# Mamba stage of a Trainium2 kernel: loop nest replaced by one list of stages with lags per engine

## The chip, the cores and the metric

The kernel runs on one NeuronCore of one Trainium2 chip. The metric is the device time of one execution in microseconds (us), lower is better. The kernel before takes 4172.57 us, the median of 3 runs (4169.62 to 4175.07). The engines are TensorE (PE, matmul), VectorE (DVE), ScalarE (ACT), GpSimd (POOL) and SyncE (SP). Each runs its own queue strictly in the order in which it was written, and they meet only at semaphores.

## The reference

The input x is (4, 1024, 128) in float32. A layer norm and a bidirectional Mamba block come first, then a transformer of 6 layers. The change is in the Mamba block alone, which computes this for a forward and for a backward (flipped) direction:

```
xp, z = split(x @ W_in.T)                      # 256 channels each
xc = silu(depthwise_conv4(xp) + b_conv)
dt, B, C = split(xc @ W_x.T)                   # 8, 16 and 16 columns
dt = softplus(dt @ W_dt.T + b_dt)
A = -exp(A_log)
# over 1024 tokens, for each of 256 channels and 16 states n:
h = h * exp(dt * A[n]) + (dt * xc) * B[n]
y = sum_n h * C[n]
y = (y + xc * D) * silu(z)
out = y @ W_out.T                              # x + 0.5 * (forward + backward)
```

## The kernel before

`program` (L1283 on) runs two layer norms, then `mamba` (L101), a third layer norm, and `transformer` (L588), each in a block of its own. The last two are the same in both kernels.

`mamba` works in 8 passes, one for each sequence (4) and direction (2). In a pass the tokens lie along the free dimension (1024) and the channels on the partitions, in two halves h of 128. A pass has 16 steps, one for each state n, and `g` counts steps through all passes (128 in all). One step is:

- PE spreads row B[n] over 128 partitions into a pair of PSUM banks (`b_rows`) and row C[n] into the other pair (`c_rows`). Both are the instruction of L209, two matmuls of 512 columns each.
- DVE forms the drive of half 0 in SBUF (L393) and that of half 1 in place in PSUM (L395), and scans each half over 1024 tokens (L411, `tensor_tensor_scan`, 128x1024).
- ACT has computed exp(dt * A[n]) for both halves up to 4 steps ahead (`decays`, L309) and copies the C row to SBUF (L316).
- POOL multiplies state by C row (L425), and PE adds this product to y in PSUM by a matmul with the identity (`add_read`, L229), four matmul instructions of 512 columns in the trace for each half.

PSUM has 8 banks: 4 hold y of the two halves, and the other 4 are two "slots" of two banks. B of step g takes slot g % 2; everything else of that step (C rows, every projection, the output) takes the other slot, two banks at a time. Whoever takes a slot waits for its last reader. So B of step g + 1 waits for whatever last read that slot in step g.

The next pass's projections are spread over the steps of this pass by the table `PROJECT_AT`: x at steps 1, 4 and 6, B/C/dt at 8, dt of each half at 9 and 10, z at 12 and 13. An x part of one bank is four taps, in the trace eight matmul instructions of 512 columns (L182); step 1 has two such banks. PE's order within a step is written in the loop: C rows, `add_read` of half 0 of the step before, output or projection, `add_read` of half 1, then B rows of the next step. ACT evaluates silu straight from PSUM (L277 for x, L281 for z) in each of five steps, among the exponentials, so tables are reloaded both ways (ACT_TABLE_LOAD). At step 1 DVE closes the pass before (`gate`): L366 adds xc * D to y, reading PSUM, and L372 multiplies by silu(z). At step 2 PE projects the output (L238) and DVE adds it to the residual (L380).

## Time and profile before

| | us |
|---|---|
| median of 3 runs | 4172.57 |
| the profiled execution | 4178.99 |
| its span | 4176.9 |
| first drive of step 0 (L393) starts | 115.22 |
| last scan (L411) ends | 1217.45 |
| last add to the residual (L380) starts | 1231.12 |

A time is read as us from the start of the span. A row of a group of instructions has its busy time, the mean of one in ns, the number (x), and, behind the bar, how long the engine sat idle just before such instructions and who ended that. One float32 matmul of 512 columns appears as two MATMUL instructions. The Mamba stage takes the first 1232 of 4177 us; the rest is the third norm and the transformer.

### The profile page before, as it was taken

To read this page: it belongs to the slowest core of one execution; us is meant where nothing else is said; L and a number is where in the kernel's file an instruction comes from. 1 tells how busy PE (TensorE), PEld (TensorE's weight loads), DVE (VectorE), ACT (ScalarE), POOL (GpSimd) and SP (SyncE) were. 2 spreads that over 40 slices of the span, in tenths; PEclk is the share of its full clock that TensorE was granted. 3 is DMA by queue.
4 is the path that set the end of the run, shared out by engine and by line. 5 is a ranking of instruction groups with operands and counts; after the bars stand their busy time and mean duration, and the time that the engine had idled before them with its cause. 6 is when DMAs were issued, how large, how long until landed. Compare 5 with 4: busy or idle time off the path is not lost.

```text
span 4176.9 us, 110200 instructions
## 1 busy us (share of the span) xinstructions
PE 3828.7 (92%) x43616; PEld 2570.0 (62%) x43616; DVE 3409.8 (82%) x3480; ACT 3048.1 (73%) x6956; POOL 3035.9 (73%) x2330
## 2 busy tenths in 40 slices
PE   6788888888875999999999999999999999999998
PEld 2333333333333777777777777777777777777775
DVE  3788888888975888788887888788887888788885
ACT  4655645564534888788887888788887888788885
POOL 0455555554546888888888888888888888888883
PEclk8888898898887999999999999999999999999999
DMA  1000000000000000000000000000000000000001
GB/s 41 0 1 0 0 0 0 0 0 0 0 20 32 13 2 15 2 6 13 15 3 2 16 2 15 2 6 12 2 15 2 16 2 15 2 6 2 3 2 42
DMA packets 12012, 34.46 MB, mean 8 GB/s; under 512 B 2405, under 2 KB 4329, under 8 KB 10609
## 3 DMA queue, kind: packets, MB, share of 16 engines
q1 hardware_dynamic: 11504, 27.41, 1.9%
q8 instruction: 353, 5.78, 0.6%
q14 instruction: 155, 1.26, 0.1%
HBM read 23.21 MB, written 4.19 MB: 7 GB/s over the span
## 4 chain that ended last, share of the span: by engine, by line
PE 64%; issue 2%; ACT 1%; POOL 1%; DVE 0%; POOLq 0%; ACTq 0%; DVEq 0%
PE ps L849 16%; PE ps L779 12%; PE ps L838 9%; PE ps L790 8%; PE ps L826 6%; PE ps L874 5%; PE ps L887 3%; PE ps L811 1%; PE ps L801 1%; PE ps L856 1%; PE ps L862 1%; ACT prob L980 0%; PE ps L761 0%; ACT mixed L989 0%; POOL resid L1257 0%
## 5 line engine op out<-in xcount | busy, mean ns | idle before, releaser
L425 POOL TENSOR_TENSOR read<-state,c_row 128x1024 f32<-128x1024 f32 x256 | 598.9, 2359 | 620.7 <-DVE state L411 501.0
L1235 POOL TENSOR_TENSOR resid<-resid,sq 128x1024 f32<-128x1024 f32 x384 | 909.8, 2375 | 4.0 <-DVE sq L1089 3.7
L1257 POOL TENSOR_TENSOR resid<-resid,rnorm 128x1024 f32<-128x1024 f32 x384 | 725.5, 1905 | 17.8
L849 PE MATMUL ps<-mixed,w_vo 128*128 128x128 f32 x6144 | 718.6, 275 | 3.0 <-ACT mixed L989 2.3
L849 PEld LDWEIGHTS ps<-mixed,w_vo 128*128 128x128 f32 x6144 | 709.6, 192 | 12.9 <-issue 4.6
L779 PE MATMUL ps<-w_qk,xs_parts 128*128 128x512 f32 x2304 | 641.3, 414 | 47.3 <-issue 18.2
L980 ACT ACTIVATE prob<-ps,stat 128x64 f32<-128x64 f32 x3072 | 653.3, 384 | 1.1 <-DVE stat L1109 1.1
L229 PE MATMUL mamba_ps<-read,ident 128*128 128x512 f32 x1024 | 572.0, 697 | 22.4 <-DVE xc L366 19.8
L1089 DVE TENSOR_TENSOR sq<-ps,rope_l 128x1024 f32<-128x1024 f32 x384 | 462.7, 1205 | 119.1 <-ACT sq L942 118.8
L1102 DVE TENSOR_TENSOR resid<-ps,rope_l 128x1024 f32<-128x1024 f32 x384 | 464.5, 1210 | 74.6 <-ACT sq L942 67.5
L779 PEld LDWEIGHTS ps<-w_qk,xs_parts 128*128 128x128 f32 x2304 | 414.8, 192 | 164.0 <-issue 81.1
L942 ACT ACTIVATE sq<-ps 128x1024 f32<-128x1024 f32 x384 | 395.7, 1030 | 162.3 <-PE ps L779 127.0
L1264 POOL TENSOR_TENSOR prob<-prob,stat 128x1024 f32<-128x1024 f32 x192 | 366.2, 1907 | 174.9 <-DVE stat L1120 174.8
L989 ACT COPY mixed<-ps 128x512 f32<-128x512 f32 x768 | 399.5, 601 | 110.5 <-PE ps L838 110.5
L1066 DVE TENSOR_REDUCE ssq<-sq 128x16 f32<-128x1024 f32 x384 | 465.7, 1213 | 8.1 <-ACT sq L942 3.7
L790 PE MATMUL ps<-ident,resid 128*128 128x128 f32 x3072 | 413.9, 274 | 14.3 <-ACT w_vo L924 13.1
L229 PEld LDWEIGHTS mamba_ps<-read,ident 128*128 128x128 f32 x1024 | 209.1, 217 | 311.6 <-issue 262.1
L790 PEld LDWEIGHTS ps<-ident,resid 128*128 128x128 f32 x3072 | 350.9, 141 | 75.8 <-issue 61.1
L838 PE MATMUL ps<-prob_t,rows 32*128 32x512 f32 x3072 | 383.8, 613 | 4.2 <-DVE xb L1137 1.6
L316 ACT COPY c_row<-mamba_ps 128x1024 f32<-128x1024 f32 x128 | 128.4, 1003 | 270.9 <-PE mamba_ps L209 270.9
L964 ACT COPY q_t<-ps 128x512 f32<-128x512 f32 x384 | 230.4, 600 | 124.0 <-PE ps L790 121.7
L826 PE MATMUL ps<-k_t,q_t 64*32 64x64 f32 (+1 forms) x24576 | 291.6, 225 | 9.8 <-issue 9.3
(139 smaller groups left out, 6158.5 us busy)
## 6 DMA issues: line engine op xcount, KB each, us to landing
w_stage<-w_qk_hbm SPq DMA_DIRECT2D x6, 1024.0 KB, 4.9
vo_stage<-w_v_hbm SPq DMA_DIRECT2D x6, 512.0 KB, 3.8
vo_stage<-w_o_hbm SPq DMA_DIRECT2D x6, 512.0 KB, 4.6
xn<-x_hbm SPq DMA_DIRECT2D x4, 512.0 KB, 5.3
kept<-resid SPq DMA_DIRECT2D x8, 256.0 KB, 3.1
resid<-kept SPq DMA_DIRECT2D x8, 256.0 KB, 4.5
out_hbm<-resid SPq DMA_DIRECT2D x8, 256.0 KB, 2.0
w_stage<-w_hbm SPq DMA_DIRECT2D x6, 341.0 KB, 2.9
```

What stands on the lines that cost most here:

```text
L229: last = pe.matmul(y_ps[h][:, c, :], ident[:, :], read[:, (2 * g + h) % 4, c * BANK:(c + 1) * BANK], start=n == 0, stop=n == D_STATE - 1)
L425: pool.tensor_tensor(read[:, u % 4, :], state[:, u % 4, :], c_row[:, (u // 2) % 2, :], ALU.mult).then_inc(read_ready, 1)
L779: last = pe.matmul(ps[:, A + c, :], xs_parts[:, odd, xpart, :], w_qk[:, wpart, cols], start=k == 0, stop=k == 2)
L790: last = pe.transpose(bank[:, j * P:(j + 1) * P], qk[:, tile % 2, col:col + P], ident[:, :])
L826: last = pe.matmul(ps[w * WINDOW:(w + 1) * WINDOW, S + h, first:(a + 1) * 2 * WINDOW], q_t[rows_h, odd, a, w * WINDOW:(w + 1) * WINDOW], k ...
L838: last = pe.matmul(banks[w], rows[rows_w, tile % 2, own, :], prob_t[rows_w, tile % 2, :, own, :], start=own == 0, stop=own == 1)
L849: last = pe.matmul(bank[:, 0:P], w_vo[:, l % 2, head_at(place_h), :], mixed[:, odd, place_h, :], start=place_h == 0, stop=place_h == HEADS ...
L980: last = act.activation(prob[:, tile % 2, place_h, :], score_ps[:, place_h, :], ACT.Exp, bias=stat[:, tile % 2, 0, place_h:place_h + 1])
L1066: dve.tensor_reduce(ssq[:, tile % 2, part * HEADS:(part + 1) * HEADS, 0], sq[:, 0, :].rearrange("p (h d) -> p h d", d=HEAD_DIM), AX_X, ALU ...
L1102: dve.tensor_tensor(qk[:, tile % 2, part * INNER:(part + 1) * INNER].rearrange("p (h d) -> p h d", d=HEAD_DIM), heads_ps.rearrange("p (h d ...
L1235: pool.tensor_tensor(qk[:, tile % 2, cols], qk[:, tile % 2, cols], sq[:, 1 + part, :], ALU.add).then_inc(done[f"rotated{part}"], 1)
L1257: pool.tensor_tensor(heads, heads, norms, ALU.mult).then_inc(done[f"normed{part}"], 1)
```

## The change

Each engine's work in `mamba` is now one list of entries (lag, step, name): `MAMBA_PE`, `MAMBA_ACT`, `MAMBA_DVE`, `MAMBA_POOL`. `mamba_sequence` runs over iterations i and emits every entry for pass i - lag, so that entries of lag 1 and 2 belong to earlier passes than those of lag 0. Waits are made from the producers' counts (`after`). Names: `b` B rows, `c0`/`c1` C row by bank, `x`/`z`/`dt`/`bc` projections (half, bank), `sk` skipped input, `y` the add into y, `o` output by bank; on ACT `a...` takes a bank, `sx`/`sz` silu, `ex`/`ln` softplus, `dec` decay, `cc` copy of C; on DVE `dr` drive, `sc` scan, `gm` gate, `ao` add output, `ar`/`tx` the two steps of dt.

- Banks: B still takes a pair of two banks, alternating with the step. Everything else takes a single bank of the other pair, in turn (`mamba_slots`), and waits only for that bank's last reader. So C rows, projections and outputs, and their readers on ACT and DVE, are in pieces of 512 columns.
- The skipped input xc * D is no longer added by DVE. ACT makes 4 diagonal matrices `skip` once, and PE starts y with the matmul of `skip` and xc (8 more MATMUL instructions a pass).
- The gate on DVE is one multiply per half that reads y from PSUM.
- ACT takes x and z out of PSUM by Identity or Copy in 512 columns, and applies silu later in SBUF on 1024 columns. The exp/ln table is preloaded after a silu, so that Exp and Ln use one table.
- The semaphore `stored` moves out of `transformer`.

```diff
+def mamba_slots(pe):
+    slots, last, turn, pair = {}, [None] * 4, [0, 0], 1
+    for name, k in pe:
+        if name == "b":
+            pair = k % 2
+            banks, reader = [2 * pair, 2 * pair + 1], ("sc1", k)
+        elif name in single:
+            other = 1 - pair
+            banks, reader = [2 * other + turn[other]], (single[name], k)
+            turn[other] ^= 1
...
+MAMBA_PE = [
+    (2, 12, "c0"), (2, 13, "b"), (0, None, "x01"), (2, 11, "y0"), (2, 13, "c1"), (2, 14, "b"), (2, 13, "c0"),
...
-                def gate(s):
-                    d = s % 2
-                    for h in range(HALVES):
-                        dve.wait_ge(summed, 2 * (D_STATE * (s + 1) - 1) + h + 1)
-                        dve.scalar_tensor_tensor(out=xc[:, d, h, :], in0=xc[:, d, h, :],
-                                                 scalar=packed[:, d, D_SKIP + h:D_SKIP + h + 1],
-                                                 in1=y_ps[h], op0=ALU.mult, op1=ALU.add).then_inc(skip_added, 1)
-                    for h in range(HALVES):
-                        dve.wait_ge(skip_added, HALVES * s + h + 1)
-                        dve.wait_ge(zs_ready, HALVES * s + h + 1)
-                        dve.tensor_tensor(zs[:, d, h, :], xc[:, d, h, :], zs[:, d, h, :], ALU.mult).then_inc(gated_ready, 1)
+                def gate(h):
+                    def stage(s):
+                        after(dve, (f"y{h}", D_STATE * s + LAST), (f"sz{h}", s))
+                        x = zs[:, s % 2, h, :].rearrange("p (c n) -> p c n", c=HALF_BANKS)
+                        dve.tensor_tensor(x, y_ps[h], x, ALU.mult).then_inc(done[f"gm{h}"], 1)
...
+                def add_skip(h):
+                    def stage(s):
+                        after(pe, (f"sx{h}", s), (f"gm{h}", s - 1))
+                        for c in range(HALF_BANKS):
+                            last = pe.matmul(y_ps[h][:, c, :], skip[:, s % 2, h, :], xc[:, s % 2, h, cols(c)],
+                                             start=True, stop=False)
...
+                def silu(letter, tile):
+                    def half(h):
+                        def stage(s):
+                            after(act, *[(f"a{letter}{h}{c}", s) for c in range(HALF_BANKS)])
+                            x = tile[:, s % 2, h, :]
+                            act.activation(x, x, ACT.Silu).then_inc(done[f"s{letter}{h}"], 1)
...
+                for i, (name, k) in enumerate(ACT_SEQ):
+                    stages[name](k)
+                    tables = [x[0] for x in ACT_SEQ[i + 1:] if x[0] in MAMBA_EXPS + MAMBA_SILUS]
+                    if name in MAMBA_SILUS and tables and tables[0] in MAMBA_EXPS:
+                        act.preload_act_table_set("natural_log_exp_and_others")
```

First place: PE in steps 4 to 5 of a pass, where one bank of the next pass's x is projected. The kernel before, from the C rows of step 4 to the B rows of step 5:

```order
L209 MATMUL mamba_ps<-bc,pick_r 128x512 [waits state_ready]
L209 MATMUL mamba_ps<-bc,pick_r 128x512
L229 MATMUL mamba_ps<-read,ident 128x512 [waits read_ready]
L229 MATMUL mamba_ps<-read,ident 128x512
L182 MATMUL mamba_ps<-xn,wtap 128x512 [waits c_copied]
L182 MATMUL mamba_ps<-xn,wtap 128x511
L182 MATMUL mamba_ps<-xn,wtap 128x510
L182 MATMUL mamba_ps<-xn,wtap 128x509
L229 MATMUL mamba_ps<-read,ident 128x512 [waits read_ready]
L229 MATMUL mamba_ps<-read,ident 128x512
L209 MATMUL mamba_ps<-bc,pick_r 128x512 [waits xc_ready]
L209 MATMUL mamba_ps<-bc,pick_r 128x512
```

The changed kernel at the same place (L310 are the rows of B and C, L279 the x projection, L341 the add into y; `m_sc` is counted by the scans, `m_cc` by the C copies, `m_ax` by ACT's taking of x):

```order
L310 MATMUL mamba_ps<-bc,pick_r 128x512 [waits m_sc,m_split]
L279 MATMUL mamba_ps<-xn,wtap 128x512 [waits m_sc]
L279 MATMUL mamba_ps<-xn,wtap 128x512 x3
L310 MATMUL mamba_ps<-bc,pick_r 128x512 [waits m_cc,m_split]
L341 MATMUL mamba_ps<-read,ident 128x512 [waits m_rd]
L341 MATMUL mamba_ps<-read,ident 128x512
L310 MATMUL mamba_ps<-bc,pick_r 128x512 [waits m_cc,m_ax,m_split]
L310 MATMUL mamba_ps<-bc,pick_r 128x512
```

Between the scan's release and the B rows of the next step there stands one add of a half less, and the projection no longer waits for the copy of C.

Second place: DVE where a pass is closed, in steps 1 and 2 of the next one. The scan of L411 is printed as SCALAR_TENSOR_TENSOR. The kernel before, from the drives of step 1:

```order
L393 TENSOR_TENSOR drive<-dtx,mamba_ps 128x1024 [waits state_ready,b_ready]
L395 TENSOR_TENSOR mamba_ps<-dtx,mamba_ps 128x1024 [waits drive_ready]
L366 SCALAR_TENSOR_TENSOR xc<-xc,packed,mamba_ps 128x1024 [waits summed] x2
L372 TENSOR_TENSOR zs<-xc,zs 128x1024 [waits zs_ready,skip_added] x2
L411 SCALAR_TENSOR_TENSOR state<-decay,drive 128x1024 [waits read_ready,drive_ready,decay_ready]
L411 SCALAR_TENSOR_TENSOR state<-decay,mamba_ps 128x1024 [waits read_ready,drive_ready,decay_ready]
```

The changed kernel, from the gate (L503) to the first half of the output (L516); L487 is the drive, L495 the scan:

```order
L503 TENSOR_TENSOR zs<-mamba_ps,zs 128x1024 [waits m_sz,m_y] x2
L487 TENSOR_TENSOR drive<-dtx,mamba_ps 128x1024 [waits m_sc,m_tx,m_b]
L487 TENSOR_TENSOR mamba_ps<-dtx,mamba_ps 128x1024 [waits m_tx,m_b]
L495 SCALAR_TENSOR_TENSOR state<-decay,drive 128x1024 [waits m_rd,m_dr,m_dec]
L516 SCALAR_TENSOR_TENSOR resid<-mamba_ps,resid 128x512 [waits m_o]
L495 SCALAR_TENSOR_TENSOR state<-decay,mamba_ps 128x1024 [waits m_rd,m_dr,m_dec]
```

The gate is two instructions instead of four, stands ahead of the drives of step 1 instead of behind them, and waits for the last add into y; the output comes in two halves, the second of them three steps later.

## Rows read from the trace of the kernel before

**Rows 1.** The page, part 1: busy time, share of the span, instructions.

```profile
PE 3828.7 (92%) x43616; PEld 2570.0 (62%) x43616; DVE 3409.8 (82%) x3480; ACT 3048.1 (73%) x6956; POOL 3035.9 (73%) x2330
```

**Rows 2.** Windows: length, busy of each engine, PEclk, DMA share, GB/s.

```profile
253.00:391.00 138.00, 117.87 (x253) 47.54 (x253) 119.38 (x75) 78.92 (x75) 74.84 (x32) 0.90 0.00 0
942.00:1079.00 137.00, 116.97 (x241) 47.11 (x241) 114.08 (x70) 72.58 (x69) 70.19 (x30) 0.86 0.00 0
1133.00:1168.00 35.00, 30.92 (x58) 12.10 (x58) 34.48 (x21) 15.48 (x15) 23.86 (x12) 0.80 0.00 0
...
2500.00:3000.00 500.00, 492.18 (x7341) 380.23 (x7340) 420.82 (x494) 417.17 (x1112) 429.61 (x368) 0.99 0.03 8
```

**Rows 3.** Waits of DVE, 115 to 1218: total, times, longest.

```profile
DVE drive L393 <- PE mamba_ps L209: 125.3, 54, 7.0
DVE resid L380 <- PE mamba_ps L238: 15.0, 7, 2.3
```

**Rows 4.** Timeline of DVE: start, length, instruction.

```profile
1133.05 1.19 DVE L393 TENSOR_TENSOR drive<-dtx,mamba_ps 128x1024 f32<-128x1024 f32 x1
1137.78 2.25 DVE L411 TENSOR_TENSOR_SCAN state<-decay,mamba_ps 128x1024 f32<-128x1024 f32 x1
1139.95 1.19 DVE L393 TENSOR_TENSOR drive<-dtx,mamba_ps 128x1024 f32<-128x1024 f32 x1
```

**Rows 5.** Timeline of DVE where pass 0 is closed in pass 1.

```profile
257.51 2.46 DVE L366 SCALAR_TENSOR_TENSOR xc<-xc,packed,mamba_ps 128x1024 f32<-128x1024 f32 x2
259.90 2.35 DVE L372 TENSOR_TENSOR zs<-xc,zs 128x1024 f32<-128x1024 f32 x2
272.21 1.22 DVE L393 TENSOR_TENSOR drive<-dtx,mamba_ps 128x1024 f32<-128x1024 f32 x1 [5.58 <-PE mamba_ps L209]
```

**Rows 6.** Timeline of PE, steps 4 to 6 of pass 1.

```profile
297.10 1.20 PE L209 MATMUL mamba_ps<-bc,pick_r 64*128 64x512 f32 x4
298.22 3.70 PE L229 MATMUL mamba_ps<-read,ident 128*128 128x512 f32 x8
301.85 0.73 PE L209 MATMUL mamba_ps<-bc,pick_r 64*128 64x512 f32 x2
304.77 0.73 PE L209 MATMUL mamba_ps<-bc,pick_r 64*128 64x512 f32 x2 [2.19 <-DVE state L411]
305.43 1.98 PE L229 MATMUL mamba_ps<-read,ident 128*128 128x512 f32 x4
307.25 3.60 PE L182 MATMUL mamba_ps<-xn,wtap 128*128 128x512 f32 x8
310.69 1.88 PE L229 MATMUL mamba_ps<-read,ident 128*128 128x512 f32 x4
...
320.18 0.73 PE L209 MATMUL mamba_ps<-bc,pick_r 64*128 64x512 f32 x2 [2.21 <-DVE state L411]
320.83 3.49 PE L229 MATMUL mamba_ps<-read,ident 128*128 128x512 f32 x4
```

**Rows 7.** Groups of instructions, of which DVE's 115 to 1233.

```profile
L425 POOL TENSOR_TENSOR read<-state,c_row 128x1024 f32<-128x1024 f32 x256 | 598.9, 2359 | 620.7 <-DVE state L411 501.0
L309 ACT ACTIVATE decay<-dt,neg_a 128x1024 f32<-128x1024 f32 x256 | 279.7, 1142 | 0.5
L309 ACT ACT_TABLE_LOAD x43 | 55.2, 1283 | 0.8
L989 ACT COPY mixed<-ps 128x512 f32<-128x512 f32 x768 | 399.5, 601 | 110.5 <-PE ps L838 110.5
L395 DVE TENSOR_TENSOR mamba_ps<-dtx,mamba_ps 128x1024 f32<-128x1024 f32 x128 | 157.2, 1228 | 4.4
L366 DVE SCALAR_TENSOR_TENSOR xc<-xc,packed,mamba_ps 128x1024 f32<-128x1024 f32 x16 | 19.8, 1275 | 4.5 <-PE mamba_ps L229 4.5
```

**Rows 8.** Timeline of the end of the stage.

```profile
1215.20 2.25 DVE L411 TENSOR_TENSOR_SCAN state<-decay,mamba_ps 128x1024 f32<-128x1024 f32 x1
1225.74 5.34 PE L238 MATMUL mamba_ps<-zs,wout 128*128 128x512 f32 x8 [2.60 <-DVE zs L372]
```

More of the change, by code:

```diff
@@ L258, in _, with free, project_x @@
-                for h in range(HALVES):
-                    add_read(STEPS - 1, h)
-                output(PASSES - 1, other_slot(STEPS - 1))
+                pe.wait_ge(skip_ready, 2 * HALVES)
+                def free(name, k):
+                    after(pe, *SLOTS[name, k][1])
+                    return bank(name, k)
+                def project_x(h, c):
+                    def stage(s):
+                        to, d = free(f"x{h}{c}", s), s % 2
+                        for tap in reversed(range(D_CONV)):
+                            skip = max(0, D_CONV - 1 - tap - c * BANK)
+                            seen = tokens(s, c * BANK + skip - (D_CONV - 1 - tap), BANK - skip)
+                            last = pe.matmul(to[:, skip:], wtap[:, d, tap, h * P:(h + 1) * P], seen,
+                                             start=tap == D_CONV - 1, stop=tap == 0)
+                        last.then_inc(done[f"x{h}{c}"], 1)
+                    return stage
@@ new lines, in b_rows, with c_rows, stage @@
+                def b_rows(g):
+                    after(pe, ("split", g // D_STATE))
+                    free("b", g)
+                    for c in range(HALF_BANKS):
+                        last = rows(pair(g)[:, c, :], g, g % D_STATE, c)
+                    last.then_inc(done["b"], 1)
+                def c_rows(c):
+                    def stage(g):
+                        after(pe, ("split", g // D_STATE))
+                        rows(free(f"c{c}", g), g, D_STATE + g % D_STATE, c).then_inc(done[f"c{c}"], 1)
+                    return stage
@@ new lines, in take_bc, with stage, round_bc @@
+                def take_bc(c):
+                    def stage(s):
+                        after(act, (f"bc{c}", s), ("split", s - 1), *[(f"dt{h}{k}", s - 1) for h in range(HALVES) for k in range(2)])
+                        act.copy(x_dbl[:, cols(c)], bank(f"bc{c}", s)[0:BC_ROWS + DT_RANK]).then_inc(done[f"abc{c}"], 1)
+                    return stage
+                def round_bc(s):
+                    after(act, ("abc0", s), ("abc1", s), ("b", D_STATE * (s - 1) - 1), ("c0", D_STATE * (s - 1) - 1),
+                          ("c1", D_STATE * (s - 1) - 1))
+                    act.copy(bc[:, s % 2, :], x_dbl[0:BC_ROWS, :]).then_inc(done["abch"], 1)
@@ L429 @@
+                stages = halved("rd", read_out)
+                for name, k in POOL_SEQ:
+                    stages[name](k)
 DEPTH, HEADS, HEAD_DIM, WINDOW = 6, 16, 64, 32
```

439 lines of the change are left out of this document (210 added, 229 removed), and 43 rows, old and new, of tables (MAMBA_ACT, MAMBA_DVE, MAMBA_PE, MAMBA_POOL).

## Prediction, made before the changed kernel ran

> **What bounds the kernel now.** I read the page's first part, then the busy time by stretches, DVE's waits, and DVE's and PE's timelines of single steps. Over the whole program PE is busy 92% [rows 1], which misleads here: in the transformer, which is unchanged, it is busy 492 of 500 us at a granted clock of 0.99, but in the Mamba stage only 117 of 137 or 138 us at 0.86 to 0.90 [rows 2]. The change touches the Mamba stage alone.
>
> There the scan engine sets the pace. A step on DVE (two drives, two scans) takes 1139.95 - 1133.05 = 6.90 us when nothing is late [rows 4], and in the last pass, where PE has no projections to do, DVE is busy 34.5 of 35 us [rows 2], although the granted clock was only 0.80. In the other passes DVE is late: from the first drive to the last scan it waits 125.3 us for B rows in 54 cases and 15.0 us for the output, 140.3 us together [rows 3], or 17.5 us for each of 8 passes of (1217.45 - 115.22) / 8 = 137.8 us. So two ceilings matter: DVE's own work, and what PE can do in that time.
>
> **DVE's work after.** 128 steps stay: 128 x 6.90 = 883 us. The seven gates inside the loop lose two additions of the skipped input; the two of them take 259.90 - 257.51 = 2.39 us [rows 5], so 7 x 2.39 = 16.7 us go. The remaining multiply now reads one operand from PSUM. The drive of half 1 does just that at 1.228 us [rows 7], against 1.18 for the old one (half of 2.35) [rows 5]: I charge nothing. The output in two pieces costs a second start; the trace shows no such piece in this form, so I bound it by nothing and by a whole instruction of 1.275 us as L366's [rows 7], take 0.25, and 7 x 0.25 = 2 us.
>
> **The waits that go.** Take the x projection [rows 6]. After the scan's release at 304.77 PE does C rows, one add (1.8), the x part (3.44), a second add (1.8); B rows come at 312.49 at the earliest, 7.7 us later, then 0.7 for themselves: more than the 6.90 that DVE takes. The new order has C half row 0.3, x 3.44, half row 0.3, one add 1.8, B rows 0.65: 6.5 us. It fits with 0.4 us to spare. Step 1 holds a double x part of 7.4 us and DVE waits 5.58 there [rows 5]; it is broken into single banks in separate steps. Splitting banks also means that PE need not wait for the copy of C ahead of a projection. I count all 140.3 us as freed, and then charge new ones:
> - The gate. It now stands ahead of the drives of step 1 and waits for the last add into y. From the end of the last scan of the pass: C copied after 2 us, two products on POOL at 2.36 each [rows 7] end at 6.7, the last add (1.8 us) at 8.5 to 9.7. DVE reaches the gate at 6.9 and its second half at 8.1. I charge 1.5 us; bounds 0 and 3.
> - Tight places. By the same count of the lists, B rows are ready 0.1 to 0.5 us ahead of need in some five places of a pass (x11 and x00 with the skip, the B/C projection, the softplus). A handoff that is longer, or PE at the lower clock for one x part (twice 3.44 us), turns this into a stall of up to 3 us. I charge 3 us a pass; bounds 0 and 7.
> That is 4.5 us in each of seven passes, 31, and 5 us in pass 0, whose first x part meets a PE that has idled: 36 us, bounds 0 and 75.
>
> **Does PE carry it?** PE's work at full clock, from [rows 6]: adds 16 x 3.63 = 58.1 us (298.22 to 301.85); B and C rows 16 x 1.2 = 19.2; x 4 x 3.44 = 13.8; z, B/C, dt and output, 8 instructions each at 0.44, 14.2; the new skip, 8 x 0.44 = 3.5. Together 108.8 us a pass, 3.5 of them new. DVE's pass is 16 x 6.90 + 9.7 = 120.1 us (the 9.7: split, two sums, two products, two gates, outputs, about 1.2 each). PE is at 91%, so the skip is covered as long as the clock is granted; without cover it costs 8 x 3.5 = 28 us.
>
> **The clock.** It was 0.86 to 0.90 over a pass [rows 2], and this can be seen in place: after an idle 2.21 us the four instructions at 320.83 spread over 3.49 us, while after an idle 2.19 us those at 305.43 took 1.98 [rows 6]. So waits of this length stand ahead of the lower of the two levels (1.2 of 2.4 GHz) only now and then. In the transformer, where PE hardly waits, the clock is 0.99 [rows 2]. The new order leaves PE fewer idle stretches than now, so I take a value between the 0.89 of now and that 0.99: about 0.95.
> The Trainium skill speaks against the change here: "TensorE: Matmul & The Clock Gate", section "A second HAM failure mode: psum-queue depth-cycling", says that a PE which cycles through PSUM banks idles in small bits between groups often enough for its clock to swing. By that rule, more and smaller bank turns would give no better clock than now; the sum above needs 0.91 or more. Rows of this kernel's transformer do not bear it out, and rows of its Mamba stage partly do, which is the first rival.
>
> **Other engines.** ACT per pass: 32 decays at 1.09 is 35 us, 32 half copies at 0.60 is 19, 8 table loads at 1.283 is 10 [rows 7] (88 loads stood in the stage, 43 of them ahead of the decays; the new order has 62), the rest about 21: 86 of 120 us. The halves' price is from a 512-column copy of the transformer [rows 7]. POOL: 32 x 2.36 = 75.5 us. Neither binds; decays are up to four steps ahead, which hides the silu pairs and the extra pass over SBUF. Were that cover gone, two table loads (2.6 us) would show at each of 4 places a pass.
>
> **Start and end.** Before the first drive, ACT's exp/ln switches drop out of the chain (two loads, 2.6 us) and a separate silu comes in (1.1): -2 us, bounds -5 and +3. At the end the add of the skip (1.28) and half of the serial products (1.2) drop out, and the residual is added in halves: -2.8 us of 14.9 [rows 8].
>
> **The sum.** -140.3 - 16.7 + 2 + 36 - 2 - 2.8 = -123.8 us. The profiled execution took 4178.99 us, so 4055.2; it was 6.4 us above the median of the runs, so about 4049 in their terms. With the bounds of the stalls alone: 4013 to 4088.
>
> **Rivals.**
> 1. PE becomes the bound. If the clock stays at 0.885, PE needs 108.8 / 0.885 = 123 us a pass, and with some 5 us of waits that its fixed order forces on it (for the scan that frees a pair), 128. Against 137.8 that is 8 x 9.8 = 78 us, with start and end 83: 4090 us. For it: the clock now. Against it: the last pass, where DVE never waited at 0.80 (but with a third less for PE to do).
> 2. Slower than before: the clock falls. The lists give PE a fixed order in which a C half row often waits for the scan of its own step, with adds and projections queued behind it. If such waits keep PE at the lower level more often, a pass costs 108.8 / clock; it passes today's 137.8 when the mean clock is under 0.79. At 0.75 it is 145 us, 8 x 7.3 = 58 us more: about 4230. Only the last pass shows a clock near this (0.80), and there PE had a third less to do.
> 3. The waits only move. DVE waits on products (POOL waits for adds that PE now does up to two steps late; both buffers of two are as deep as before) for as long as it waited for B rows. Then only the gate and the ends count, 20 us: 4152. Against it: POOL idles 620 us for DVE [rows 7], so it has room.
>
> **How the numbers follow.** Forecast 0.75, rival 1 0.15, rival 3 0.05, rival 2 0.05. The likeliest gives 4049. The range is 4015 (nearly no stalls) to 4105 (rival 1 with its own spread); it leaves out rivals 2 and 3 and the edges. A measurement here tells about 0.2%, 8 us, from no change. Faster: forecast, rival 1 and most of rival 3, 0.94; same 0.01; slower 0.05.
>
> **What would show it.** Right: passes of 122 to 126 us from gate to gate; DVE's waits for B rows under 40 us; scans still 2.25 to 2.35 us; a granted clock of 0.93 or more; gates waiting 1 to 2 us for PE; 62 table loads. Wrong: a step without extras over 6.9 us, DVE waiting for POOL or for decays, PE busy without gaps at a clock under 0.9, or any change in the transformer's span of about 2945 us behind the stage.

## The result, and the profile after

The changed kernel takes 4141.14 us (median of 4 runs, 4138.62 to 4142.07), the kernel before 4173.55 in the same runs: a ratio of 0.992, with a 95% interval of 0.9906 to 0.9934. It is faster, but by 32 us (0.8%) and not by the 124 that were forecast, and it lies outside the predicted range. The kernel before had medians of 4173.55 to 4175.43 us in the four sets of runs of this document, so a difference between two kernels of different sets is uncertain by some 2 us.

The span fell from 4176.9 to 4136.8 us, by 40.1. From the timelines: the first drive starts 3.1 us earlier (115.22, now 112.08), the time from the first drive to the end of the last scan fell by 30.6 (1102.2, now 1071.6), from there to the end of the last residual add by 2.7 (14.9, now 12.2), and the rest of the program by 3.6 (2944.5, now 2940.9). So the Mamba loop is where it was decided: a pass took 134 us in place of 137.8, where 122 to 126 had been expected (first drive to last scan, divided by 8).

Windows of two passes in the middle (columns as in [rows 2]):

```profile
246.00:380.00 134.00, 122.87 (x264) 47.26 (x264) 124.70 (x74) 80.83 (x101) 86.31 (x33) 0.94 0.00 0
380.00:514.00 134.00, 122.34 (x264) 47.37 (x264) 124.89 (x74) 80.83 (x100) 86.39 (x33) 0.95 0.00 0
```

The granted clock rose to 0.94 to 0.95 from the 0.86 to 0.90 of [rows 2], as forecast. But DVE is busy 124.8 us of 134, where the prediction had counted 120.1 us of work for a whole pass, and it still waits for 9. Its waits from the first drive to the last scan:

```profile
DVE drive L487 <- PE mamba_ps L310: 57.9, 44, 4.3
DVE zs L503 <- PE mamba_ps L341: 11.9, 12, 1.2
DVE dt L472 <- ACT dt L426: 9.7, 7, 1.8
```

Against [rows 3] the waits for B rows fell from 125.3 to 57.9 us, and those for the output are gone; two new ones add 21.6. The groups of instructions: the scans, and POOL's product beside the one of [rows 7]:

```profile
L495 DVE TENSOR_TENSOR_SCAN state<-decay,drive 128x1024 f32<-128x1024 f32 x128 | 343.6, 2684 | 0.0
L495 DVE TENSOR_TENSOR_SCAN state<-decay,mamba_ps 128x1024 f32<-128x1024 f32 x128 | 290.0, 2266 | 2.9
...
L529 POOL TENSOR_TENSOR read<-state,c_row 128x1024 f32<-128x1024 f32 x256 | 684.6, 2691 | 503.2 <-ACT c_row L440 199.4 <-DVE state L495 192.7 <-PE mamba_ps L341 111.1
```

The two scans do the same arithmetic. That of half 1 takes its forced term from PSUM and kept its length. That of half 0 has both inputs, `decay` and `drive`, in SBUF, and it got longer. The same two groups in the kernel before:

```profile
L411 DVE TENSOR_TENSOR_SCAN state<-decay,drive 128x1024 f32<-128x1024 f32 x128 | 299.5, 2340 | 0.2
L411 DVE TENSOR_TENSOR_SCAN state<-decay,mamba_ps 128x1024 f32<-128x1024 f32 x128 | 289.1, 2259 | 0.0
```

A small part of the difference, 2340 against 2259 ns, was there already. POOL's product went from 2359 to 2691 ns. Single instructions show what happens (timeline, DVE and POOL, pass 0):

```profile
175.93 2.35 POOL L529 TENSOR_TENSOR read<-state,c_row 128x1024 f32<-128x1024 f32 x1 [0.68 <-PE mamba_ps L341]
176.15 4.28 DVE L495 TENSOR_TENSOR_SCAN state<-decay,drive 128x1024 f32<-128x1024 f32 x1
180.35 2.26 DVE L495 TENSOR_TENSOR_SCAN state<-decay,mamba_ps 128x1024 f32<-128x1024 f32 x1
180.51 4.69 POOL L529 TENSOR_TENSOR read<-state,c_row 128x1024 f32<-128x1024 f32 x2 [2.23 <-DVE state L495]
```

The scan starts 0.22 us after the product and has 4.28 us instead of 2.28. The product would end at 178.28, 2.13 us after the scan's start: the scan's extra 2.00 us are that time, less 0.13. The scan from PSUM beside it (180.35, with two products from 180.51 on) has its 2.26 us. Of the 128 scans of half 0, 42 are over 2.4 us, with 52 us above 2.28 in all, and in each of the 42 the extra time is what was left of the running product, less 0.13 us. Of the scans from PSUM, 63 start while a product runs, and none is over 2.29 us. In the kernel before, 44 scans of half 0 were over 2.4 us as well, by the same rule, but the longest was 2.58 us and the sum 7.7 us: there POOL's two products began when the scan of half 0 ended, ran under the scan of half 1 and the drives, and had at most 0.43 us to go when the next scan of half 0 began.

So there were two places to explain: DVE's scans held up beside POOL (theory A), and waits for B rows that the new lists left (theory A' below: a silu with its two table loads stands ahead of the copy of C that frees the bank). The rival for both (theory B, B') was that TensorE's own order and work sets a pass of 134 us, and that long scans only fill time in which B rows are late anyway.

### The profile page after: what moved, and what is told of

Read it like the earlier page. It is cut to its first block, busy times and chain, and to the rows that moved or that the text cites. A ratio compares the mean times of both kernels' runs of the same rounds, so it can differ in the third digit from the quotient of the medians.

```text
span 4136.8 us, 111854 instructions
## 1 busy us (share of the span) xinstructions
PE 3851.8 (93%) x43680; PEld 2565.3 (62%) x43680; DVE 3437.3 (83%) x3472; ACT 3062.8 (74%) x7158; POOL 3119.0 (75%) x2330
## 4 chain that ended last, share of the span: by engine, by line
PE 65%; issue 2%; ACT 2%; DVE 0%; POOL 0%; POOLq 0%; ACTq 0%; DVEq 0%
PE ps L958 16%; PE ps L888 13%; PE ps L947 9%; PE ps L899 8%; PE ps L935 6%; PE ps L983 5%; PE ps L996 3%; PE ps L920 1%; PE ps L910 1%; PE ps L965 1%; PE ps L971 1%; ACT prob L1089 0%; PE ps L870 0%; ACT mixed L1098 0%; ACT w_qk L1018 0%
## 5 line engine op out<-in xcount | busy, mean ns | idle before, releaser
L529 POOL TENSOR_TENSOR read<-state,c_row 128x1024 f32<-128x1024 f32 x256 | 684.6, 2691 | 503.2 <-ACT c_row L440 199.4
L341 PE MATMUL mamba_ps<-read,ident 128*128 128x512 f32 x1024 | 537.8, 659 | 3.3 <-POOL read L529 3.3
L899 PEld LDWEIGHTS ps<-ident,resid 128*128 128x128 f32 x3072 | 353.6, 142 | 75.3 <-issue 60.8
L440 ACT COPY c_row<-mamba_ps 128x512 f32<-128x512 f32 x256 | 146.6, 584 | 310.7 <-PE mamba_ps L310 309.7
L341 PEld LDWEIGHTS mamba_ps<-read,ident 128*128 128x128 f32 x1024 | 195.0, 205 | 250.8 <-issue 233.8
L495 DVE TENSOR_TENSOR_SCAN state<-decay,drive 128x1024 f32<-128x1024 f32 x128 | 343.6, 2684 | 0.0
```

The costliest lines, as they stand in the source:

```text
L341: last = pe.matmul(y_ps[h][:, c, :], ident[:, :], read[:, h, g % 2, cols(c)], start=False, stop=n == LAST)
L529: pool.tensor_tensor(read[:, h, g % 2, :], state[:, h, g % 2, :], c_row[:, g % 2, :], ALU.mult).then_inc(done[f"rd{h}"], 1)
L899: last = pe.transpose(bank[:, j * P:(j + 1) * P], qk[:, tile % 2, col:col + P], ident[:, :])
```

## The experiments

### The scan of half 0 from PSUM

```diff
+                        from_psum = h or COUNT["sc0", g] < COUNT["sc1", g]
...
+                        if from_psum:
+                            after(dve, ("dr1", g))
-                        force = pair(g).rearrange("p c n -> p (c n)") if h else drive[:, :]
+                        force = pair(g).rearrange("p c n -> p (c n)") if from_psum else drive[:, :]
```

> The changed kernel, but at the 12 of 16 steps in which the scan of half 0 stands ahead of that of half 1, the scan of half 0 takes its forced term from the PSUM pair (which holds half 1's drive; so half 0 gets the wrong forced term, and its own drive is computed and not used). Nothing is left out. In 4 steps of a pass the scan of half 0 still reads SBUF. Theory A (a scan with two SBUF inputs and a GpSimd product hold each other up; that costs about 50 us of stretched scans in the changed kernel): no scan of half 0 from PSUM longer than 2.4 us, GpSimd's product back from 2.69 to about 2.4 us mean, and 35 to 50 us less than the changed kernel's 4141: 4091 to 4106. Theory B (TensorE's order and the waits for B rows set the pace; long scans only fill time in which the next B rows are late anyway): the scans get short, but the waits for B rows grow by as much; under 10 us gained, 4131 to 4141. A mix: the scans' 45 us go and a third to a half of it comes back as waits for B rows, about 4115.

Measured: 4114.29 us (4112.32 to 4115.12), ratio to before 0.9859 (0.9843 to 0.9876), 27 us less than the changed kernel. The groups:

```profile
L498 DVE TENSOR_TENSOR_SCAN state<-decay,mamba_ps 128x1024 f32<-128x1024 f32 x224 | 502.5, 2277 | 17.3 <-DVE mamba_ps L487 0.5
...
L498 DVE TENSOR_TENSOR_SCAN state<-decay,drive 128x1024 f32<-128x1024 f32 x32 | 72.6, 2270 | 0.0
...
L532 POOL TENSOR_TENSOR read<-state,c_row 128x1024 f32<-128x1024 f32 x256 | 620.2, 2438 | 545.3 <-ACT c_row L440 323.7 <-PE mamba_ps L341 163.8 <-DVE state L498 57.7
```

DVE's waits from the first drive to the last scan:

```profile
DVE drive L487 <- PE mamba_ps L310: 72.9, 59, 5.5
```

No scan is stretched any more, and POOL's product came back to 2438 ns. The scan with two SBUF inputs is what clashes with POOL. In the total, this is the case called a mix: 15 us of the gain came back as waits for B rows (57.9, now 72.9). The edit also has a price of its own, which the expectation left out. Each scan of half 0 now waits for the drive of half 1 right ahead of it, and from the start of that drive to the start of the next instruction there are 1.353 us on average in place of 1.175, or 23 us over 128 steps. So the 27 us may understate what the clash costs; by how much, this run does not say. Theory A names the cause of the long scans; it is not the whole of what held the kernel.

### The same edit in the kernel before

```diff
-                    for h, force in enumerate((drive[:, :], flat[g % 2])):
+                    for h, force in enumerate((flat[g % 2], flat[g % 2])):
...
-                        dve.wait_ge(drive_ready, u + 1)
+                        dve.wait_ge(drive_ready, 2 * g + 2)
```

> The kernel before with both scans reading the PSUM pair (half 1's drive; the drive of half 0 is computed and not used, so half 0 gets the wrong forced term). Nothing is left out. It shows what the two-SBUF-input scans cost in the old order, in which GpSimd's products begin as that scan ends. Theory A (the exclusion of GpSimd and a two-SBUF scan): only 7.5 us of stretch is there to gain, and the scans now wait for the drive of half 1 that stands ahead of them anyway: 0 to -8 us, 4165 to 4173; GpSimd's products 2.3 us. If scans from PSUM had a price of their own: the scan's mean stays at 2.26 us, and no row shows more. A gain over 20 us would say that the clash costs the old order as much as the new, which would speak against it as the cause of the missed gain.

Measured: 4167.04 us (4162.71 to 4173.41, 10 runs) against 4174.85, ratio 0.9985 (0.9976 to 0.9995): 8 us. This total is a balance and not the price of the clash alone: by the timelines the stretch of 7.7 us goes and the waits for B rows fall by 16.0 us (125.3, now 109.3), but the scans now wait for the drive ahead of them, which costs 18 us. What shows that the old order had mostly avoided the clash is the rows of its scans: 7.7 us of stretch in the kernel before, 52 in the changed one.

### No tables in the loop

```diff
-                            act.activation(x, x, ACT.Silu).then_inc(done[f"s{letter}{h}"], 1)
+                            act.activation(x, x, ACT.Relu).then_inc(done[f"s{letter}{h}"], 1)
...
-                    if name in MAMBA_SILUS and tables and tables[0] in MAMBA_EXPS:
+                    if False:
```

> The changed kernel with Relu in place of the four silus of a pass and no preloading of the exp/ln table, so that no table is loaded in the loop; it leaves out the silu, all else is the same. Theory A' (copies of C that stand behind a silu with its two table loads make the B rows of steps 2 and 4 late, 1.2 and 1.5 us a pass): these two waits go, DVE's waits for B rows fall from 60 us to about 37, and the time by 15 to 25 us, to 4116 to 4126. Theory B' (TensorE's own work between the scan's release and the B rows is too long there whatever ScalarE does): waits for B rows stay at 50 us or more and the time falls by under 6 us (start only). Stretched scans of half 0 should stay at some 5 a pass by theory A of the run before, since nothing of them hangs on tables; if they go too, what puts GpSimd late is ScalarE.

Measured: 4098.05 us (4095.67 to 4099.99), ratio 0.9822 (0.9807 to 0.9836): 43 us less than the changed kernel, twice the 15 to 25 expected. DVE's waits for B rows in the loop fell from 57.9 to 34.6 us, and, which was not expected, the excess of the scans of half 0 from 52 to 39 us: it vanished at step 4 and stayed at steps 8 to 12. So part of the clash hangs on ScalarE: a late copy of C makes a product late.

### Two silus moved

```diff
-    (2, 3, "cc0"), (2, 4, "dec1"), ...
+    (2, 3, "cc0"), (1, None, "sx0"), (2, 4, "dec1"), ...
-    (1, 2, "dec1"), (1, 3, "dec1"), (1, 3, "dec0"), (0, None, "ax10"), (1, None, "sz0"), (1, 2, "cc0"),
-    (0, None, "ax00"), (1, 2, "cc1"), (1, 4, "dec0"), (1, 5, "dec0"), (1, 3, "cc1"), (0, None, "sx0")]
+    (1, 2, "dec1"), (1, 3, "dec1"), (1, 3, "dec0"), (0, None, "ax10"), (1, 2, "cc0"), (1, None, "sz0"),
+    (0, None, "ax00"), (1, 2, "cc1"), (1, 4, "dec0"), (1, 5, "dec0"), (1, 3, "cc1")]
```

> The changed kernel with two entries of ScalarE's list moved and nothing left out: the silu of z of half 0 stands behind the copy of C bank 0 of step 2 instead of ahead of it, and the silu of x of half 0 behind the copy of C bank 0 of step 3 of the next iteration, ahead of the decays of step 4. As many table loads as before. Theory A' (the two silus with their tables make the C bank late that the B rows of steps 2 and 4 wait for): most of what the run without tables gained comes back in a correct kernel, 15 to 30 us: 4111 to 4126; waits for B rows at steps 2 and 4 go. Theory B' (it is the table loads' time on ScalarE as a whole, wherever they stand): within 6 us of 4141, the waits turn up at other steps.

Measured: 4101.95 us (4096.29 to 4104.21), ratio 0.9819 (0.9803 to 0.9836). With every table load still there (67 up to the end of the stage in both), 39 us are won, more than the 15 to 30 expected, and within the uncertainty as much as the 43 of the run without tables: what costs is not the loads' time on ScalarE but what stands behind them. The stretched scans are mostly still there (42 us in all). The changed kernel at step 4 of pass 1, the place that the prediction had worked out (timeline, ACT, PE, DVE and POOL):

```profile
280.70 0.58 ACT L440 COPY c_row<-mamba_ps 128x512 f32<-128x512 f32 x1 [2.32 <-PE mamba_ps L310]
281.30 1.28 ACT L391 ACT_TABLE_LOAD   x1
282.60 1.06 ACT L391 ACTIVATE xc<-xc 128x1024 f32<-128x1024 f32 x1
...
283.67 1.28 ACT L451 ACT_TABLE_LOAD   x1
284.97 0.58 ACT L440 COPY c_row<-mamba_ps 128x512 f32<-128x512 f32 x1
...
285.65 0.92 PE L310 MATMUL mamba_ps<-bc,pick_r 64*128 64x512 f32 x3 [1.36 <-issue]
285.68 4.69 POOL L529 TENSOR_TENSOR read<-state,c_row 128x1024 f32<-128x1024 f32 x2 [0.58 <-ACT c_row L440]
286.38 1.22 DVE L487 TENSOR_TENSOR drive<-dtx,mamba_ps 128x1024 f32<-128x1024 f32 x1 [1.53 <-PE mamba_ps L310]
286.50 5.40 PE L279 MATMUL mamba_ps<-xn,wtap 128*128 128x512 f32 x8
...
288.65 3.87 DVE L495 TENSOR_TENSOR_SCAN state<-decay,drive 128x1024 f32<-128x1024 f32 x1
```

One late instruction is paid three times. The copy of C at 284.97 waited behind two loads and the silu. PE waited for it with the B rows (DVE idle 1.53 us). POOL waited for it too and started its product at 285.68, so that its second one was running when the scan came at 288.65 and held that 1.6 us. And PE, after its idle 1.36 us, ran the eight matmuls of the x part in 5.40 us, at a granted clock of 0.68, instead of the 3.60 of [rows 6]. The profile names no releaser for the B rows ("issue"); that it was the copy is read from the lists, in which these B rows wait for it, and from this run and the next, in which the waits of step 4 go with the silu. The moved kernel at step 2, ACT and DVE:

```profile
257.84 0.58 ACT L440 COPY c_row<-mamba_ps 128x512 f32<-128x512 f32 x1 [1.45 <-PE mamba_ps L310]
258.45 1.28 ACT L391 ACT_TABLE_LOAD   x1
...
259.74 1.06 ACT L391 ACTIVATE zs<-zs 128x1024 f32<-128x1024 f32 x1
260.42 1.22 DVE L487 TENSOR_TENSOR drive<-dtx,mamba_ps 128x1024 f32<-128x1024 f32 x1
260.82 1.28 ACT L451 ACT_TABLE_LOAD   x1
```

The same loads now stand behind the copy, and the drive at 260.42 waits for nothing.

### One silu moved

The edit is the part of the one above that moves `sx0`.

> The changed kernel with one entry moved: the silu of x of half 0 goes behind the copy of C bank 0 of step 3 (the silu of z of half 0 stays ahead of that of step 2). Nothing is left out. Both moves together gave 39 us, 4102 against 4141. DVE's waits for B rows were 1.2 us at step 2, 1.6 at step 3 and 1.5 at step 4 of a pass, and the scan of half 0 at step 4 was 1.6 us too long. If each silu costs by what stands at its own step: this one, with the B rows of step 4 and the long scan behind it, about 3 us a pass, 20 to 25 us: 4116 to 4121. If the two only help together (what one delays, the other hides): under 10 us, 4131 or more.

Measured: 4121.63 us (4117.11 to 4122.38), ratio 0.987 (0.9855 to 0.9885), half of the gain of both and about what was expected. Summed over the 8 passes in DVE's timeline, waits for B rows at step 4 went from 10.7 us to nothing and the excess of the scan there from 11.2 to 0.4, together 21.5; the time fell by 19.5. With `sz0` moved too, the waits at step 2 went from 11.3 to 1.5, half of the further 19.7 us. So `sx0` costs what stands at its own step; of what `sz0` costs, half is seen at its step, and the rest is spread.

### Both causes at once

The edits of the first and of the third experiment together.

> Both edits of before at once in the changed kernel: where the scan of half 0 stands first it reads the PSUM pair, and the silus are Relu without table loads (leaves out the silu; half 0 gets the wrong forced term). Alone they gave 27 us (4114 against 4141) and 43 us (4098). If the two costs are separate (stretched scans; C copies late behind tables), they add up: 4141 - 70 = 4071. If part of the 43 us came from fewer clashes, as the scans' sum that fell from 344 to 331 us in that run says, then about 12 us are counted twice: 4083. If TensorE's order limits both (theory B), it stays near 4098. DVE's waits for B rows: 40 to 50 us by the first two, over 60 by theory B.

Measured: 4074.91 us (4072.57 to 4077.72), ratio 0.9758 (0.9744 to 0.9773): 66 us less than the changed kernel, where the two edits alone add up to 70. In the profiled executions the time from the first drive to the last scan fell by 22.6 and 37.0 us with one edit and by 60.4 with both. So the two costs add up, and an overlap is not clear of the uncertainty. About 26 us were left to the forecast: in this run DVE still waits 38.7 us for B rows, and the scans still pay the 23 us of waiting for the drive ahead of them.

### What holds what: a GpSimd copy, and a product in two pieces

```diff
-                        pool.tensor_tensor(read[:, h, g % 2, :], state[:, h, g % 2, :], c_row[:, g % 2, :],
-                                           ALU.mult).then_inc(done[f"rd{h}"], 1)
+                        pool.tensor_copy(read[:, h, g % 2, :], state[:, h, g % 2, :]).then_inc(done[f"rd{h}"], 1)
```

> The changed kernel with GpSimd copying state into read, one SBUF input, in place of the product of state and C row; it leaves out the multiplication by C. If what stops the scan is any GpSimd access to SBUF, a copy of this length stretches a scan that starts during it by what is left of the copy, as the product does (rows up to 2.2 + the copy's length). If it takes two SBUF inputs on both sides, no scan of half 0 is over 2.4 us, and the time falls by the 27 us of the PSUM run or more, to 4110 or less. A copy that is itself shorter than 2.3 us would lessen the clashes in either case; then the rows of single scans decide, not the total.

Measured: one run, 4089.68 us; too little for an interval, so its rows are what counts. A copy is only 1.04 us long there when nothing holds it, and 6 scans of half 0 are over 2.4 us. All of these start when a copy has 0.81 us to go, and have 2.95 us; those that start 0.24 us before its end have 2.38. It needs no second input on POOL's side: a copy that reads SBUF holds the scan as well, for the rest of its own length, and the 52 us of excess fell to 5 because copies are short. The six extra times (0.67 us) are again what was left of the copy, less 0.14. The guess that it takes two inputs on both sides is refuted, although the time alone (under 4110) would have spoken for it.

```diff
-                        pool.tensor_tensor(read[:, h, g % 2, :], state[:, h, g % 2, :], c_row[:, g % 2, :],
-                                           ALU.mult).then_inc(done[f"rd{h}"], 1)
+                        for c in range(HALF_BANKS):
+                            last = pool.tensor_tensor(read[:, h, g % 2, cols(c)], state[:, h, g % 2, cols(c)],
+                                                      c_row[:, g % 2, cols(c)], ALU.mult)
+                        last.then_inc(done[f"rd{h}"], 1)
```

> The changed kernel with each GpSimd product in two instructions of 512 columns in place of one of 1024; nothing is left out. A 512-column product of the transformer takes 1.28 us on GpSimd, so a pair costs 2.56 against 2.36 us, 0.2 us more each. If the scan with two SBUF inputs waits for the end of the one GpSimd instruction in progress and then runs through, the longest scan of half 0 falls from 4.28 us to about 3.5 (2.28 + at most 1.2), the excess of the 128 scans from 52 us to about 25, and the time by 5 to 20 us: 4121 to 4136. If the scan waits until GpSimd has nothing ready to issue (it must lose to both halves of the product), the scans stay as long as they are, up to 4.3 us or more, and the time rises by up to 10 us: 4141 to 4151. If the two instead share the port element by element, single scans would become longer than 2.28 by an amount that does not depend on where in a GpSimd instruction they start.

Measured: 4118.18 us (4118.09 to 4118.8), ratio 0.9864 (0.9848 to 0.9881), 23 us less than the changed kernel, a little more than the 5 to 20 expected. The longest scan of half 0 is 3.35 us in place of 4.28, the excess of all 33 us in place of 52. More scans are hit, 66 over 2.4 us in place of 42, each by what was left of the running half product, less 0.13 us. So the scan waits for the end of the one POOL instruction that is running, and then runs through, even where another of POOL is ready:

```profile
169.01 25.24 POOL L530 TENSOR_TENSOR read<-state,c_row 128x512 f32<-128x512 f32 x14
...
175.55 2.56 DVE L495 TENSOR_TENSOR_SCAN state<-decay,drive 128x1024 f32<-128x1024 f32 x1
...
182.95 3.31 DVE L495 TENSOR_TENSOR_SCAN state<-decay,drive 128x1024 f32<-128x1024 f32 x1
```

### The lists in another order

Nothing but the four lists differs from the changed kernel. Two things stand out in them. In 14 of 16 steps (4 in the changed kernel) the scan of half 1, from PSUM, stands first and that of half 0 behind it:

```diff
-    (0, 2, "dr0"), (0, 2, "dr1"), (0, 2, "sc0"), (0, 2, "sc1"), (0, 3, "dr0"),
+    (0, 2, "dr0"), (0, 2, "dr1"), (1, None, "ao1"), (0, 2, "sc1"), (0, 2, "sc0"), (0, 3, "dr0"),
```

and `sz1` follows `sx1` in ScalarE's list, so that they share their table loads.

> The changed kernel with all four lists in another order and nothing else changed or left out. The order was sought by a count of the lists in which a scan of half 0 and a GpSimd product exclude each other and silus cost 1.3 us for a table on either side. If the two causes (GpSimd against the two-SBUF scan, silus ahead of C copies) are what holds the changed kernel back, and not TensorE's or GpSimd's total work, this should give 40 to 70 us: 4070 to 4100, with DVE's waits for B rows under 30 us and the scans of half 0 under 310 us in sum. If a pass of this work can't be packed much below 134 us on this chip whatever the order: 4130 or more.

Measured: 4026.56 us (4024.62 to 4033.46), ratio 0.9645 (0.9631 to 0.966), 115 us less than the changed kernel and 147 less than the one before, well beyond the 40 to 70 us expected. The windows of the same stretches of time (a pass is shorter than such a window here), the groups, and DVE's waits:

```profile
246.00:380.00 134.00, 130.15 (x292) 50.52 (x293) 128.85 (x82) 85.24 (x107) 104.44 (x36) 0.97 0.00 1
380.00:514.00 134.00, 130.15 (x292) 50.37 (x291) 128.86 (x80) 87.08 (x108) 102.20 (x36) 0.97 0.00 0
```

```profile
L496 DVE TENSOR_TENSOR_SCAN state<-decay,drive 128x1024 f32<-128x1024 f32 x128 | 292.5, 2285 | 0.0
...
L530 POOL TENSOR_TENSOR read<-state,c_row 128x1024 f32<-128x1024 f32 x256 | 752.5, 2959 | 326.7 <-DVE state L496 245.6 <-ACT c_row L441 59.4 <-PE mamba_ps L342 21.8
```

```profile
DVE drive L488 <- PE mamba_ps L311: 6.2, 11, 1.9
```

One scan of 128 is stretched, B rows are late by 6.2 us in all, and the loop takes 963.7 us (111.62 to 1075.28), 120.5 a pass, close to the 120.1 of DVE's own work in the prediction. The clash is still there, but it is POOL that pays, with products of 2959 ns and time to spare. The timeline of a step, in which the product behind the first scan is ready 0.16 us too late to come ahead of the second:

```profile
501.85 2.29 DVE L496 TENSOR_TENSOR_SCAN state<-decay,mamba_ps 128x1024 f32<-128x1024 f32 x1
504.06 2.27 DVE L496 TENSOR_TENSOR_SCAN state<-decay,drive 128x1024 f32<-128x1024 f32 x1
504.22 6.58 POOL L530 TENSOR_TENSOR read<-state,c_row 128x1024 f32<-128x1024 f32 x2 [0.47 <-DVE state L496]
```

Two products take 6.58 us here, 4.69 without the scan (180.51 above). That the order of the two scans alone would do it was not tried. The new lists also have fewer table loads, 53 up to the end of the stage in place of 67.

With the tables taken out of these lists as well, by the edit shown under "No tables in the loop":

> The reordered lists (4026.6 us) with Relu in place of the silus and no table loads; it leaves out the silu. In the changed kernel the same edit gave 43 us. If the reordered lists gained by taking tables off the path that B rows wait for, the edit now gives under 10 us: 4017 to 4027, most of it in the prologue (1 or 2 loads ahead of the first drive, 1.3 us each). If ScalarE's total load still counts: 4010 or less.

Measured: 4025.13 us (4024.51 to 4031.79), ratio 0.9645 (0.963 to 0.9659), within the spread of the run with them. What was worth 43 us in the changed kernel is worth nothing where the loads stand in no one's way.

### The gate and the diagonal alone, in the kernel before

```diff
-                    if n == 0 and s:
-                        pe.wait_ge(skip_added, HALVES * (s - 1) + h + 1)
+                    if n == 0:
+                        if s:
+                            pe.wait_ge(gated_ready, HALVES * (s - 1) + h + 1)
+                        pe.wait_ge(xc_ready, len(X_PARTS) * (s + 1))
+                        for c in range(HALF_BANKS):
+                            pe.matmul(y_ps[h][:, c, :], skip[:, s % 2, h, :], xc[:, s % 2, h, c * BANK:(c + 1) * BANK],
+                                      start=True, stop=False)
...
-                        dve.tensor_tensor(zs[:, d, h, :], xc[:, d, h, :], zs[:, d, h, :], ALU.mult).then_inc(gated_ready, 1)
+                        x = zs[:, d, h, :].rearrange("p (c n) -> p c n", c=HALF_BANKS)
+                        dve.tensor_tensor(x, y_ps[h], x, ALU.mult).then_inc(gated_ready, 1)
```

> The kernel before with one part of the change alone: the skipped input goes through TensorE as a diagonal matrix, and the gate is one multiply that reads y from PSUM; loops, slots and order stay as they are. Nothing is left out. By the working of the prediction: two DVE instructions of 1.2 us less in each of 7 passes inside the loop (-16.7 us), 8 more TensorE instructions of 0.44 us a pass (+3.5 us a pass) at step 0, and -1.3 to -2 us in the tail. If TensorE's extra work hides (theory A): 4173 - 18 = 4155. If TensorE is late there and its 3.5 us a pass show (theory B): 4173 - 18 + 28 = about 4183. If DVE's saved time only turns into waiting for the B rows of step 2 (theory C): within 6 us of 4173.

Measured: 4225.94 us (4222.11 to 4227.89), ratio 1.0127 (1.0112 to 1.0142): 51 us slower than before, beyond each of the three cases. But the timelines divide the span's 43 us (4176.9, now 4220.2) in two. The Mamba stage ends only 9.6 us later (last residual add, 1232.35, now 1241.94), close to the 10 us later of theory B. The other 33.8 us stand behind the stage (2944.5, now 2978.3), where the code is the same. DVE's waits, and then the timeline of PE and DVE where pass 0 is closed, show what happens in the stage:

```profile
DVE drive L401 <- PE mamba_ps L212: 163.3, 57, 11.4
```

```profile
263.84 3.78 PE L233 MATMUL mamba_ps<-xc,skip 128*128 128x512 f32 x4 [2.78 <-DVE zs L380]
...
269.46 7.02 PE L185 MATMUL mamba_ps<-xn,wtap 128*128 128x512 f32 x16
276.31 1.88 PE L233 MATMUL mamba_ps<-xc,skip 128*128 128x512 f32 x4
...
280.60 1.22 DVE L401 TENSOR_TENSOR drive<-dtx,mamba_ps 128x1024 f32<-128x1024 f32 x1 [11.31 <-PE mamba_ps L212]
```

The eight new matmuls stand in the one step that already held the double x part: the waits of step 2 over all passes went from 40.7 to 83.1 us. In pass 1 the wait went from 5.58 ([rows 5]) to 11.31 us: from its first matmul after the gate to the B rows PE now takes 16.0 us in place of 12.6, and DVE arrives some 2.3 us earlier. From the first drive to the last scan DVE works 17 us less and waits 31 us more, so that this stretch takes 13.9 us longer; the end of the stage gains 5.6 and the start loses 1.3. A saving of 16.7 us on DVE, put into PE's most crowded step, made the loop slower. The lists break up the double x part, so the same work may cost less in them; what it costs there by itself was not tried.

Behind the stage, most of the 33.8 us is idle time of PE. Its largest part stands ahead of one group of matmuls of the transformer, for which the profile names no releaser (the kernel before, then this run):

```profile
L826 PE MATMUL ps<-k_t,q_t 64*32 64x64 f32 (+1 forms) x24576 | 291.6, 225 | 9.8 <-issue 9.3
L834 PE MATMUL ps<-k_t,q_t 64*32 64x64 f32 (+1 forms) x24576 | 292.2, 225 | 31.8 <-issue 31.8
```

No run shows why. In the profiled executions of the other twelve kernels the part behind the stage took 2935.1 to 2944.5 us. An edit of one stage can thus change the time of another that it does not touch, and a total alone would have put all 51 us down to the skip.

## Why the prediction was right in direction and wrong in size

Its sum, for the loop, against what the timelines give (us; the spacing of an instruction, from its start to that of the next without the idle time):

| term | predicted | measured |
|---|---|---|
| waits that go, less the stalls left in the loop | -140.3 + 36 = -104.3 | -140.3 + 79.5 = -60.8 |
| gates | -16.7 | -16.2 |
| output in pieces | +2 | about 0 |
| SBUF scans and the DVE sums with two SBUF inputs, held by POOL | 0 | 47.1 + 7.8 + 1.9 = +56.8 |
| drive of half 1 no longer waits for that of half 0 | 0 | -10.7 |
| start, end | -2, -2.8 | -3.1, -2.7 |

The measured loop terms add up to -30.9, against the 30.6 us by which it fell. Point by point:

- **The step that failed first** is "128 steps stay: 128 x 6.90 = 883 us". It took the length of a scan as a property of the instruction. It is one of where POOL stands: 2.28 us alone, up to 4.28 beside a product. The old order mostly kept the two apart; POOL's releaser in [rows 7], "DVE state L411 501.0", says so: its products began when a scan ended, the clash-free moment. I read that row as room on POOL, not as an order worth keeping. But the sign could be seen before the change: the two groups of scans do the same work, and that with both inputs in SBUF had a mean of 2340 ns against 2259, with 44 scans over 2.4 us. The prediction shows neither group. The Trainium skill had the rule: "SBUF — State Buffer", section "🔬 SBUF: two separate sides", says that a DVE instruction with two SBUF inputs and a GpSimd instruction that reads SBUF take the pair of ports they share as an exclusive lock, and whichever starts first has it for the whole instruction. The rows agree in each point: 4.28 us for a scan, 6.58 for two products held by one, 2.26 for the scan from PSUM, and 2.95 beside a plain copy.
- **The second is "Other engines":** "decays are up to four steps ahead, which hides the silu pairs". For the decays this holds; DVE never waited for one. It overlooked that the copies of C stand in the same queue and have no such lead: they free the bank that PE needs. The prediction's own price, 2.6 us at each of 4 places a pass, was not used. The silus at two of these places are worth 39 us. A late copy also makes POOL late, and so feeds the first cause.
- **The term of stalls** (36 us, bounds 0 to 75) measured 79.5: 57.9 for B rows, 11.9 for the gate, 9.7 for ScalarE's logarithm of dt. The 6.5 us for PE at step 4 held as a count, but "0.4 us to spare" assumed a C copy in time and PE at the higher of its two clock levels; the x part took 5.40 us at a granted clock of 0.68.
- **Right:** the clock (0.95 forecast, 0.94 to 0.95 measured in the middle passes, 0.93 over the whole loop with its start), the 62 table loads of the stage, the gate (1.221 us each from PSUM, waiting 1.0 us on average), start and end, DVE's floor of 120 us a pass, which the reordered lists reach, and the lookahead that frees PE from the old waits. Of the rivals, PE as the bound was named with 128 us a pass; a pass of 134 was none of the three, and the reordered lists, with the same work on PE in 120.5 us a pass, refute it. Rival 3 (4152) lies nearer to the measured time than the forecast, but by its number alone: the waits did not merely move, they fell by 61 us, and half of that went into longer instructions.
- **"Passes of 122 to 126", "waits under 40", "scans still 2.25 to 2.35 us"** were the signs to watch; all three failed, and the third named the cause.

What stays open: how the 115 us of the reordered lists divide between the two causes. The scan from PSUM and the missing tables give 66 together; in that run DVE still waited 38.7 us for B rows, in the reordered lists 6.2, but which of the many moves freed them was not taken apart. Open as well is why the program behind the Mamba stage, with the same code, took 3.6 us less in the changed kernel's profiled run (2940.9 against 2944.5 us), and 33.8 us more in the run with the gate and the diagonal alone.

## What to carry to other kernels

- A duration read from one order holds for that order only. Before giving two engines new positions, ask which pairs of instructions now overlap for the first time. In this kernel a GpSimd product or copy and a scan with two SBUF inputs did not overlap. A scan with one input in PSUM was not held, and where the clash stays, the engine with slack should be the one that starts second.
- In a queue, ask of each long instruction (here two table loads around a silu, 3.6 us) who is behind it and has no lead. Moving two entries of a list behind the copies of C was worth 39 us, more than the whole change (32).
- Work moved to another engine is priced in the step where it lands, and the whole program's time is split by stage before a cause is given to it.
- An experiment's edit can have a price of its own. Here a scan that waits for the instruction right ahead of it starts some 0.2 us later, 23 us over the run.

## What the runs showed of the hardware that was not expected

- A scan with both inputs in SBUF that starts while a GpSimd product runs is held until that instruction's end (2.28 to 4.28 us); a product that starts while such a scan runs is held too (two of them 6.58 us in place of 4.69). Scans with a PSUM operand do not change (2.25 to 2.29 us, in every run). A GpSimd instruction half as long halves the worst case (3.35 us), and the kernel gained 23 us by it.
- In the changed kernel a table load is followed by its function after 0.02 us (load at 281.30 for 1.28 us, silu at 282.60): here a switch costs its load and nothing beyond that the trace shows.
- A scan that waits for the drive right ahead of it starts 1.31 to 1.35 us after that drive's start, one that does not wait for it 1.13.
